# Three of the four blocks of a dense layer on fp16 pairs, with scales that the kernel works out itself

## The reference, cut to what matters

```
h = ln(ln(x, pw_g[id], pw_b[id]), cp_g[cid], cp_b[cid])
t = ln(x, tm_g[cid], tm_b[cid]);  s = ln(x, ms_g[sid], ms_b[sid])
m, n, r = x + mlp_ln(state of the batch)          # one row per batch each
w = softmax(aw)
cat = concat(w0 h, w1 t, w2 m, w3 n, w4 r, w5 s)
out = x + ln(silu(cat @ int_W1 + b1) @ int_W2 + b2) * g + be
```

## Time and profile before

| | before |
|---|---|
| time, median of 3 runs | 871.07 us (868.79 to 872.23) |
| profiled execution | span 867.6 us |
| PE busy | 836.8 us, 96% |
| DVE, POOL, ACT busy | 646.7, 605.7, 487.6 us |
| mean granted TensorE clock | 0.989 |

### The profile page before, as it was taken

One profiled execution on the slowest core, in us unless ns is written; L12 is line 12 of the kernel. 1 busy time (PEld: TensorE's weight loads), 2 busy tenths in 40 slices (PEclk: granted clock), 3 DMA queues, 4 the chain that ended last, 5 costly groups with the idle time before them and its releaser, 6 DMA issues.

```text
span 867.6 us, 19685 instructions
## 1 busy us (share of the span) xinstructions
PE 836.8 (96%) x7456; PEld 731.9 (84%) x7474; DVE 646.7 (75%) x1067; ACT 487.6 (56%) x851; POOL 605.7 (70%) x766
## 2 busy tenths in 40 slices
PE   5996999999999999999999999999999999999997
PEld 5853888988889898888989898888988898898986
DVE  3589778778786867678797877679797767677652
ACT  3567555565656465465656556465647546464531
POOL 2367998778786767768776866668787775756472
PEclk9998999999999999999999999999999999999999
DMA  8972233424343333525243332424343342323110
GB/s 277 419 268 62 71 91 105 126 63 150 83 151 81 98 93 86 128 51 158 71 149 89 107 93 69 127 68 145 83 123 91 87 117 49 104 68 83 47 50 25
DMA packets 104365, 95.55 MB, mean 110 GB/s; under 512 B 72880, under 2 KB 78160, under 8 KB 102608
## 3 DMA queue, kind: packets, MB, share of 16 engines
q1 hardware_dynamic: 95056, 69.26, 27.7%
q0 software_dynamic: 4608, 16.78, 7.1%
q10 hardware_dynamic: 4608, 8.25, 2.8%
HBM read 69.60 MB, written 8.40 MB: 90 GB/s over the span
## 4 chain that ended last, share of the span: by engine, by line
PE 88%; DVE 5%; DMA 2%; POOL 2%; issue 1%; ACT 1%; ACTq 0%; another core or an unknown queue 0%; DVEq 0%; POOLq 0%
PE acc L405 43%; PE tok L405 28%; PE att L405 8%; PE xp L558 6%; PE xp L405 3%; DMA kb<-in_kb 1%; DVE stg_e L1284 1%; DMA pgb<-in_pw,pidx 1%; DVE raw_k L1170 0%; DVE W1xl L1274 0%; POOL op0l L1706 0%; DVE qt L1290 0%; POOL W2l L1710 0%; DVE q L1297 0%; DVE BD L1185 0%
## 5 line engine op out<-in xcount | busy, mean ns | idle before, releaser
L1706 POOL TENSOR_TENSOR op1l<-ytmp,op1h 128x512 fp32r<-128x512 f32 x64 | 89.8, 1403 | 20.1 <-ACT op1h L912 19.6
L1652 POOL TENSOR_TENSOR xlo<-xraw,xhi 128x512 fp32r<-128x512 f32 x31 | 40.5, 1306 | 68.0 <-ACT xhi L804 68.0
L405 PE MATMUL acc<-op0h,W1xh 128*128 128x256 f32 x256 | 75.8, 296 | 1.4 <-DVE op0l L1376 1.1
L405 PE MATMUL acc<-op1h,W1th 128*128 128x256 f32 x256 | 75.0, 293 | 0.0
L405 PE MATMUL acc<-op1h,W1hh 128*128 128x256 f32 x256 | 73.7, 288 | 0.0
L405 PE MATMUL acc<-op0h,W1sh 128*128 128x256 f32 x256 | 73.7, 288 | 0.0
L405 PE MATMUL acc<-op1h,W1tl 128*128 128x256 f32 x256 | 72.4, 283 | 0.0
L405 PE MATMUL acc<-op1l,W1hh 128*128 128x256 f32 x256 | 72.4, 283 | 0.0
L405 PE MATMUL acc<-op1l,W1th 128*128 128x256 f32 x256 | 72.4, 283 | 0.0
L405 PE MATMUL acc<-op0h,W1sl 128*128 128x256 f32 x256 | 72.4, 283 | 0.0
L405 PE MATMUL acc<-op1h,W1hl 128*128 128x256 f32 x256 | 72.4, 283 | 0.0
(11 more groups left out here) (269 smaller groups left out, 3005.2 us busy)
## 6 DMA issues: line engine op xcount, KB each, us to landing
xsq<-in_x SPq DMA_DIRECT2D x32, 256.0 KB, 3.1
xb<-in_x SPq DMA_DIRECT2D x32, 256.0 KB, 3.0
out<-xb SPq DMA_DIRECT2D x32, 256.0 KB, 2.4
BD<-q SPq DMA_DIRECT2D x124, 64.0 KB, 2.1
BD<-v SPq DMA_DIRECT2D x124, 64.0 KB
xraw<-in_xT SPq DMA_DIRECT2D x30, 256.0 KB, 3.0
ring<-in_k_wT ACTq DMA_DIRECT2D x6, 256.0 KB, 3.3
dmb<-dm_rows SPq DMA_DIRECT2D x6, 256.0 KB, 3.9
```

The costliest lines, as they stand in the source:

```text
L405: return e.matmul(o, a, b, start=start, stop=True, skip_group_check=True)
L1652: e.tensor_tensor(xlo[:, :, :], (xraw1 if g == 1 else xraw)[:, :, :], xhi[:, :, :].bitcast(F32), ALU.subtract).then_inc(s["xlo"], 1)
L1706: e.tensor_tensor(op[slot]["l"][:, :, half(g)], four(ytmp[YT[n, g][0]]), op[slot]["h"][:, :, half(g)].bitcast(F32), ALU.subtract).then_inc ...
```

## The change

Blocks t, s and h, weights and operands, become fp16 pairs; x stays fp32r. The raw blocks keep a place of their own, and the high and low fp16 parts lie beside them. `op` has three slots: x and the silu, t and h, and s alone.

fp16 has a narrow range, so the kernel scales. ACT squares and sums each raw block and the gain table (`norm_of`, `accum_out` into `wn`), PE adds over the partitions (`norms`), DVE and POOL make a factor `beta` for the weights and a power of two `alpha` for the gain tables (`norms_out`, `inverse_norms`, `power_of_two`, `scales`). The three raw blocks are multiplied by `beta` (`scaled` on POOL for t and s, `scaled_h` on ACT). The x operand and the table `PT` are multiplied by `up = alpha * beta`, and the silu is taken with `scale=down = 1 / up`.

```
-        for n in "xtsh":
-            W1[n, "h"] = at(f"W1{n}h", [128, 4, 512], F32R)
+        raw = {n: at(f"raw_{n}", [128, 4, 512]) for n in "tsh"}
+        for n in "tsh":
+            for p in "hl":
+                W1[n, p] = at(f"W1{n}{p}", [128, 4, 512], F16)
-        op = [{p: at(f"op{i}{p}", [128, 4, 256], F32R) for p in "hl"} for i in range(2)]
+        op = [{p: at(f"op{i}{p}", [128, 4, 256], F16 if i else F32R) for p in "hl"} for i in range(3)]
+        op_of = {"x": op[0], "t": op[1], "s": op[2], "h": op[1]}
+        junk = at("junk", [128, 2048], BF16, offset=place["xb2"])
+        alpha, beta, up, down = nrm[:, 4:5], nrm[:, 2:3], nrm[:, 5:6], nrm[:, 6:7]
...
             e.dma_start(stg["a"][:, :, :], A["int_w1"][3]).then_inc(s["c_rn"], 16)
+            e.wait_ge(s["wn"], 4)
             load_tok(2)
...
+            def norms():
+                e.wait_ge(s["wn"], 4)
+                o = bank(("nb", 0))
+                for i in range(3):
+                    mm(o[:, 0:1], cst[:, 56:57].to_broadcast([128, 128]), wn[:, i:i + 1], start=(i == 0))
+                mm(o[:, 1:2], cst[:, 57:58].to_broadcast([128, 128]), wn[:, 3:4]).then_inc(s["nst"], 1)
...
             scores(1)
+            norms()
             out_proj(0)
...
-                e.copy(op[0]["h"][:, :, half(g)], four(xp[XP["x", g][0]])).then_inc(s["oxh"], 1)
+                    e.wait_ge(s["nst"], 6)
+                e.activation(op[0]["h"][:, :, half(g)], four(xp[XP["x", g][0]]), ACT.Copy, scale=up).then_inc(s["oxh"], 1)
...
-                elif n == "s":
-                    e.wait_ge(s["W1x"], 2 * k + 2)
+                elif n == "s" and k:
+                    e.wait_ge(s["W1s"], 2 * k)
...
-                e.activation(y[:, :], y[:, :], ACT.Silu).then_inc(s["sil"], 1)
+                e.activation(y[:, :], y[:, :], ACT.Silu, scale=down).then_inc(s["sil"], 1)
...
+            def norm_of(n):
+                e.wait_ge(s["c_r" + n], 16)
+                i = "tsh".index(n)
+                e.wait_ge(s["wn"], i + 1)
+                e.activation(junk[:, :], raw[n][:, :, :].rearrange("p a b -> p (a b)"), ACT.Square, scale=2.0 ** -15, accum_out=wn[:, i:i + 1]).then_inc(s["wn"], 1)
...
+            def scaled_h():
+                e.wait_ge(s["nst"], 9)
+                w = raw["h"][:, :, :].rearrange("p a b -> p (a b)")
+                e.activation(w, w, ACT.Copy, scale=beta).then_inc(s["nst"], 1)
...
+            def scaled(n):
+                e.wait_ge(s["Pm"], 3)
+                w = raw[n][:, :, :].rearrange("p a b -> p (a b)")
+                e.tensor_scalar(w, w, beta, None, ALU.mult).then_inc(s["nst"], 1)
+            def inverse_norms():
+                e.wait_ge(s["nst"], 2)
+                e.tensor_tensor(nrm[:, 2:4], nrm[:, 0:2], mh.to_broadcast([128, 2]), ALU.pow).then_inc(s["nst"], 1)
+            def scales():
+                e.wait_ge(s["nst"], 4)
+                e.tensor_tensor(gsc[:, :], cst[:, 5:8], alpha.to_broadcast([128, 3]), ALU.mult).then_inc(s["nst"], 1)
+                e.tensor_tensor(up, beta, alpha, ALU.mult).then_inc(s["nst"], 1)
+                e.wait_ge(s["nst"], 6)
+                e.tensor_tensor(down, up, cst[:, 22:23], ALU.pow).then_inc(s["nst"], 1)
...
             add_ob(0)
+            inverse_norms()
             true_scale(1)
+            scales()
             add_ob(1)
+            scaled("t")
+            scaled("s")
             root1(0)
```

More of the change, by code:

```diff
@@ L133, in build @@
             WL["o", p] = at(f"Wo{p}", [128, 4, 512], F16)
-        raw = {n: at(f"raw_{n}", [128, 4, 512], offset=place[f"W1{n}l"]) for n in "xtsh"}
+        raw["x"] = at("raw_x", [128, 4, 512], offset=place["W1xl"])
         raw |= {n: at(f"raw_{n}", [128, 4, 512], offset=place[f"W{n}l"]) for n in "2k"}
@@ L911, in prod_hi @@
                 e.wait_ge(s["p" + n], g + 1)
-                e.copy(op[slot]["h"][:, :, half(g)], four(ytmp[YT[n, g][0]])).then_inc(s[f"o{n}h"], 1)
+                e.copy(op_of[n]["h"][:, :, half(g)], four(ytmp[YT[n, g][0]])).then_inc(s[f"o{n}h"], 1)
             def w_copy(g):
@@ L976, in _ @@
             e.copy(t2[:, 0:256].bitcast(BF16), tr[:, :]).then_inc(s["tp"], 1)
+            e.wait_ge(s["tp"], 1)
+            e.activation(junk[:, 0:512], t2[:, 0:256].bitcast(BF16), ACT.Square, scale=2.0 ** -7, accum_out=wn[:, 3:4]).then_inc(s["wn"], 1)
             e.wait_ge(s["tA"], 1)
@@ L1043, in _ @@
             e.wait_ge(s["pa"], 1)
-            e.copy(t2[:, 0:256].bitcast(BF16), rp[:, :]).then_inc(s["tp"], 1)
+            e.activation(t2[:, 0:256].bitcast(BF16), rp[:, :], ACT.Copy, scale=up).then_inc(s["tp"], 1)
             exponential(2)
@@ L1703, in prod_lo, with lo_16 @@
             def prod_lo(g, n):
-                slot = 0 if n == "s" else 1
                 e.wait_ge(s[f"o{n}h"], g + 1)
-                e.tensor_tensor(op[slot]["l"][:, :, half(g)], four(ytmp[YT[n, g][0]]), op[slot]["h"][:, :, half(g)].bitcast(F32), ALU.subtract).then_inc(s[f"o{n}l"], 1)
+                e.tensor_tensor(op_of[n]["l"][:, :, half(g)], four(ytmp[YT[n, g][0]]), op_of[n]["h"][:, :, half(g)], ALU.subtract).then_inc(s[f"o{n}l"], 1)
+            def scaled(n):
+                e.wait_ge(s["Pm"], 3)
+                w = raw[n][:, :, :].rearrange("p a b -> p (a b)")
+                e.tensor_scalar(w, w, beta, None, ALU.mult).then_inc(s["nst"], 1)
+            def lo_16(n, sem, kts=range(4)):
+                for kt in kts:
+                    i = e.tensor_tensor(W1[n, "l"][:, kt, :], raw[n][:, kt, :], W1[n, "h"][:, kt, :], ALU.subtract)
+                if sem:
+                    i.then_inc(sem, 1)
+            def inverse_norms():
[5 more added lines that the diff above has]
+                e.tensor_tensor(up, beta, alpha, ALU.mult).then_inc(s["nst"], 1)
+                e.wait_ge(s["nst"], 6)
+                e.tensor_tensor(down, up, cst[:, 22:23], ALU.pow).then_inc(s["nst"], 1)
             def split_lo(dst, src, hi, sem, kts=range(4)):
@@ L1750, in _ @@
             e.wait_ge(s["Pm"], 3)
-            split_lo(W1["t", "l"], raw["t"], W1["t", "h"], s["wlp"])
+            lo_16("t", s["wlp"])
             root1(1)
@@ L1779, in _ @@
                 if k == 1:
-                    split_lo(W1["h", "l"], raw["h"], W1["h", "h"], None, (1,))
+                    lo_16("h", None, (1,))
                 elif front:
@@ L1788, in _ @@
                 if k == 1:
-                    split_lo(W1["h", "l"], raw["h"], W1["h", "h"], s["wlp"], (2,))
+                    lo_16("h", s["wlp"], (2,))
                 prod_lo(pa, "h")
@@ L1798, in _ @@
                 if k == 1:
-                    split_lo(W1["h", "l"], raw["h"], W1["h", "h"], s["wlp"], (3,))
+                    lo_16("h", s["wlp"], (3,))
                 if front:
@@ L1912 @@
     cst[:, 20:23] = -0.5, 0.5, -1
+    cst[:, 56] = 1
+    cst[:, 57] = gain["t"] | gain["s"] | gain["h"]
     cst[:, 24:56] = p[:, None] % 32 == np.arange(32)[None]
```

87 lines of the change are left out of this document (55 added, 32 removed).

## The result

| | before | after |
|---|---|---|
| time, median (range) | 871.16 us (868.79 to 872.23, 4 runs) | 856.04 us (855.85 to 856.82, 4 runs) |
| span of the profiled execution | 867.6 us | 853.7 us |
| mean granted TensorE clock | 0.989 | 0.982 |

The changed kernel is faster by 1.6%: ratio 0.984, 95% interval 0.9825 to 0.9854. The forecast was 852.6 us, with a range of 845.5 to 860.5. The sign and the main term are right, but 3.4 us of the gain forecast are missing. The medians differ by 15.1 us, the profiled spans by 13.9; I work with the spans. A span belongs to one execution. In nine executions of the kernel before, run beside e1 to e4, the time lies 1.8 to 1.9 us above the execution's own span, so the traced one with 867.6 us was some 1.7 us quicker than the median, and differences of a microsecond between two traces need a second witness.

A forecast was written before the change was run, and what follows sets the result against it. PE alone was taken to bound the main loop, POOL's queue the prologue. -23.1 (matmuls) + 2.0 (POOL prologue) + 1.4 (loop scales) + 1.2 (u_T waits) = -18.5 us, from 871.1 to 852.6 us; range 845.5 to 860.5.

The forecast's parts named there:

- The matmul term: PE, blocks t, s and h: each 256-column matmul falls from 120 to 109.3 ns, over 15 iterations, -23.1 us.
- The rivals of no gain and of 98 ns: PE matmuls stay at 120 ns, 874.5 us, chance 0.04; or weight load sets 98 ns, 828 us, chance 0.03.
- POOL in the prologue: Before root1(0): small operations and two passes of 2.6 us overfill POOL's idle 5.23 us; with the DVE meeting +2.0 us.
- my upper bound of 5.23: POOL in the prologue: a pass costs at most four two-stream additions of 512 columns, 5.23 us.
- the 7 us that I had named as the sign of being wrong there: Prologue: a loss of over 7 us would show the forecast wrong.
- My upper end: POOL in the prologue: with passes of 5.2 us POOL is free at 75.9 and the loss is 6.4 us.
- the first rival: POOL's prologue passes cost as much as two streams, 5.2 us each: loss 6.4 us, 857 us, chance 0.15.
- The meeting with DVE: Prologue: a DVE operation with two SBUF operands meets POOL's passes where they begin, 0.6 us.
- ACT and PE in the prologue: Sums of squares and norms make DVE's chain to root1(0) 0.9 us late, beside POOL's own 1.4 us.
- Scales in the loop: x1_hi, x1_lo and silu slow by reading a scale; PE waits 0.15 us in about nine iterations, +1.4 us.
- Waits at u_T: Loop iterations with modulation: PE reaches u_T sooner than the h chain, 0.36 us of wait, half of six taken, +1.2 us.
- From span to median: Whole kernel: the median of the runs stays 3.5 us above the profiled span.

The follow-up runs named there:

- e1: Changed kernel without POOL's two passes that multiply t and s by beta (h still is): 847.61 us, ratio 0.9743 to the kernel before.
- e4: Changed kernel with fp16 pairs for t, s and h but no norms, factors, passes or loop scales: 847.65 us, ratio 0.9747 to the kernel before.
- e3: Kernel before, fp32r throughout, with two POOL passes over t and s by a factor of one added ahead of root1(0): 877.96 us, ratio 1.0096.
- e2: Changed kernel with the passes over t and s moved from POOL to ACT, ahead of each rounding: 849.16 us, ratio 0.9776 to the kernel before.
- e8: e2 with block x on scaled fp16 pairs as well, no pass added: 844.19 us, ratio 0.9699 to the kernel before.

## Why the prediction was right, and where it was not

**The matmul term** (-23.1 us) is right. The distance fell to 109.1 ns against 109.3, an iteration is 1.48 us shorter, and e4, which has nothing else, gains 22.1 us. The rivals of no gain and of 98 ns are out.

**POOL in the prologue** (+2.0 us) failed at one step: "One read stream is nearer to none than to two full ones with their sum; I take 2.6 us." The pass takes 5.44, above even my upper bound of 5.23. I argued from the number of streams and placed a TENSOR_SCALAR that no row showed between rows of other kinds. The loss of 8.1 us is also beyond the 7 us that I had named as the sign of being wrong there. My upper end was added up wrongly besides: 75.9 less 69.31 is 6.6, and with the 0.6 for DVE 7.2, not 6.4, so the first rival should have read 857.8 us. Its mechanism (chance 0.15) is what happened; that 856.0 lies so near its 857 is in part luck, as errors of both signs follow below. Of the 7.2 us between the forecast end of the passes (70.7) and the real one (77.9), 5.7 are the price. The other 1.6 is the start, 67.1 instead of 65.5: `true_scale(1)` began 1.4 us later, and the three small operations ahead of `add_ob(1)` took 1.4 us together, where I had 1.5 for all four with a part of it hidden. By that `root1(0)` is 8.6 us late, and `u_T` 8.1.

**The meeting with DVE** (0.6 us) did not happen in this kernel. e3 shows it: 3.5 us for the DVE operation, of which 0.44 us reach POOL's chain. The kind was right; and chance decided that it was not met.

**The granted clock in the prologue** was not in my sum, and fell from 0.90 to 0.67 between 80 and 100 us. It lies where PE mostly waits: from `root1(0)` to the first `u_T` it is 59.7 us before and 59.2 after. But that stretch holds the first iteration's shorter matmuls too, and in e4, which has them, it is 58.5; so up to 0.7 us may be the clock's and all else together.

**ACT and PE in the prologue** (0.9 us beside POOL's chain) is right for DVE's chain: 0.6 us at `root1(0)` in e1. But POOL got more of it than my 0.4 us: its first low parts of the output weights start at 52.58 us instead of 50.37, and at 50.77 in e4, which has no sums of squares on ACT.

**Scales in the loop** (+1.4 us) were right in kind and too dear: "So PE will wait there, 0.15 us in about nine iterations." It is 0.12 us in six, and 0.17 at the last block, 0.9 us by the rows of e2 and e7. The 0.15 us from the end of `x1_lo` to PE's first x matmul, from which I took the size, are still there in e7, with the quicker operations. They are a fixed step and no measure of what a longer `x1_lo` costs.

**Waits at u_T** (+1.2 us) were too dear. In the iterations with modulation the hand shrank from 0.67 to 0.40 us (425.2 us after), and PE waits at one `u_T`, 0.45 us at 806.36. The loop gained 22.0 where 20.5 were forecast.

One part of why the chains kept up is on POOL, where I had put nothing. Groups of the changed kernel:

```profile
L1764 POOL TENSOR_TENSOR op1l<-ytmp,op1h 128x512 f16<-128x512 f32 x64 | 80.8, 1262 | 23.1 <-ACT op1h L932 22.6
L1764 POOL TENSOR_TENSOR op2l<-ytmp,op2h 128x512 f16<-128x512 f32 x32 | 37.5, 1172 | 12.9 <-ACT op2h L932 12.8
```

The same low parts took 1403 and 1295 ns before, which makes 13 us of POOL's loop time. That this is why the waits stayed away is argued, not tried.

**From span to median**: "The median of the runs is 3.5 us above that span, and this stays" failed. It is 2.3 us for the changed kernel, since the 3.5 held the luck of one quick traced execution. The missing 3.4 us are thus 6.1 us more lost in the prologue, less 1.5 more gained in the loop and 1.2 here: that the measurement lies so near the forecast owes something to errors that cancelled.

## What to carry to other kernels

An operation that no row shows should not be priced by counting its streams. Keep both ends in the range, and if it is to stand on the engine that decides a stage, ask which other engine has the time: the two passes cost 8.4 us on POOL and 1.5 us on ACT (e2 less e1; 2.9 us by the two ratios). Work that a change needs once, in the prologue, is paid in full where a serial chain passes through one engine, and there it can weigh over a third of what thousands of shorter matmuls give. Each further step in the loop is worth less once other chains are met: the first three blocks gave 96% of their sum (22.1 of 23.1 us), the fourth 65% by the medians, 74% by the traces and 87% by the ratios. The best kernels here, e8 and its variants, run at 844.2 us, 12 us below the change.

## What the runs showed of the hardware

- TENSOR_SCALAR on POOL over 128x2048 fp32 takes 5.44 us, a multiplication with two operands, the second one repeated, 4.03 us, ACT's copy with a scale 2.0 us.
- A matmul of 256 columns starts every 109.1 ns in fp16 and every 119 to 120 ns in fp32r.
- A subtraction on POOL with an fp16 operand and fp16 result takes 1.17 us for 512 columns, against 1.29 with fp32r.
- A DVE operation with two SBUF operands that met a long POOL pass took 4.21 us in place of 0.74.
